# Four of 49 destination blocks summed by accumulating row gathers, b_out added to x in DRAM, finishes at uneven distances

## The reference

```python
h   = x * rsqrt(deg_out)[:, None]
agg = segment_sum(h[src], dst)                # 206250 rows of 256 numbers into 6250 sums
h   = relu((agg * rsqrt(deg_in)[:, None]) @ W + b)
gnn = h / max(norm(h), 1e-12)
mix = linear attention over all nodes, 8 heads, @ w_out + b_out
ffn = top-1 of 8 experts, capacity ceil(1.25 * 6250 / 8), two layers, 1024 hidden
```

## Time and profile before

| | |
|---|---|
| time, 3 runs | 1468.57, 1470.52, 1472.99 us; median 1470.52 |
| profiled execution, first to last instruction | 1429.1 us |
| what lies around that span (median minus span) | 41.4 us |
| busy, share of the span | PE 94%, DVE 87%, ACT 67%, POOL 45% |
| busy tenths, 40 slices of 35.7 us, PE | `4899999958999999999999999999998999899987` |
| the same, DVE | `7899999988789999999999999999976586867786` |
| granted TensorE clock, mean | 0.980 of full speed |

### The profile page before, as it was taken

How to read it: one execution, slowest core, us unless ns; L and a number is a source line. 1 busy time by engine, 2 the same in 40 slices (tenths; PEclk the granted TensorE clock), 3 DMA queues, 4 the chain that set the end, 5 groups by cost and what they waited for, 6 DMA issues and landing times. The chain is left out here.

```text
span 1429.1 us, 43152 instructions
## 1 busy us (share of the span) xinstructions
PE 1337.7 (94%) x14715; PEld 1128.4 (79%) x14717; DVE 1248.9 (87%) x2315; ACT 962.9 (67%) x2239; POOL 648.8 (45%) x645
## 2 busy tenths in 40 slices
PE   4899999958999999999999999999998999899987
PEld 3466666637899999999999999999995788889986
DVE  7899999988789999999999999999976586867786
ACT  5588888775567767677677677676663658464754
POOL 4557663062234433334433344333331676776574
PEclk9899999988999999999999999999999999999999
DMA  9211111000011111121111121111113443353220
GB/s 299 60 42 46 54 45 39 23 31 1 4 62 50 37 37 37 37 72 38 37 37 37 37 73 37 37 37 37 41 71 104 129 139 107 102 161 95 76 77 26
DMA packets 61264, 89.57 MB, mean 63 GB/s; under 512 B 10231, under 2 KB 40591, under 8 KB 61154
## 3 DMA queue, kind: packets, MB, share of 16 engines
q1 hardware_dynamic: 50032, 67.20, 13.9%
q0 software_dynamic: 11136, 21.23, 5.3%
HBM read 62.91 MB, written 34.49 MB: 68 GB/s over the span
## 5 line engine op out<-in xcount | busy, mean ns | idle before, releaser
L1621 PE MATMUL bank<-reg_b,reg_a 128*128 128x256 f16 x4802 | 642.7, 273 | 0.7 <-ACT reg_a L1206 0.7
L1206 ACT ACTIVATE reg_a<-bank 128x392 f16<-128x392 f32 x784 | 358.8, 499 | 159.2 <-PE bank L1613 154.3
L1621 PEld LDWEIGHTS bank<-reg_b,reg_a 128*128 128x128 f16 x4802 | 428.9, 97 | 42.7 <-issue 0.9
L1860 DVE TENSOR_TENSOR reg_c<-iota_v,reg_c 128x2048 f16<-128x2048 f16 (+1 forms) x298 | 432.2, 1465 | 21.6 <-PE bank L1613 11.2
L845 POOL COPY key_deg<-deg_k 128x1 f32 (+1 forms) x49 | 105.0, 2143 | 463.0 <-DVE reg_c L1989 463.0
L1613 PE MATMUL bank<-reg_a,reg_c 128*128 128x98 f16 x3136 | 261.4, 208 | 6.1 <-DVE reg_e L2069 2.2
L1613 PEld LDWEIGHTS bank<-reg_a,reg_c 128*128 128x128 f16 x3136 | 213.5, 98 | 24.9 <-issue 7.9
L1860 DVE TENSOR_TENSOR reg_a<-iota_h,reg_c 128x1568 f16<-128x1568 f16 x196 | 215.7, 1101 | 0.0
L1816 PE MATMUL bank<-w_hi,hid_hi 128*128 128x256 f32 (+1 forms) x368 | 107.3, 292 | 12.7 <-DVE w_lo L2342 7.5
L1818 PE MATMUL bank<-w_hi,hid_lo 128*128 128x256 f32 (+1 forms) x368 | 104.6, 284 | 0.0
L1817 PE MATMUL bank<-w_lo,hid_hi 128*128 128x256 f32 (+1 forms) x368 | 104.5, 284 | 0.0
(11 more groups left out here) (360 smaller groups left out, 2529.4 us busy)
## 6 DMA issues: line engine op xcount, KB each, us to landing
reg_b<-in_L_ffn_w SPq DMA_DIRECT2D x16, 1024.0 KB
tok_rows<-reg_e SPq DMA_DIRECT2D x24, 512.0 KB, 3.8
x_t<-in_x SPq DMA_DIRECT2D x24, 256.0 KB
xnT_t<-xnT_rows SPq DMA_DIRECT2D x24, 256.0 KB, 2.9
...
```

The source lines that it names most:

```text
L1206: return a.activation(AT[k].rearrange("p h (w t) -> p h w t", w=2)[:, :, :, s * GROUP:(s + 1) * GROUP], tile_ps[bk][:, 0:GROUP * 2 * NB].r ...
L1621: ins = t_.matmul(agg_ps[k][:, 0:D], AT[k][:, h, :], h_all[:, h, half * D:(half + 1) * D], start=(first and h + half == 0), stop=(last and ...
L1860: return v_.tensor_tensor(out.rearrange("p t (v u) -> p t v u", u=2), iota.rearrange("p (v u) -> p v u", u=2).unsqueeze(1).to_broadcast(sh ...
```

## The change

Four things change together.

- **Gathered blocks.** If no node needs an extra round, blocks 16, 17, 32 and 33 (pairs 8 and 16, `GATHERED`) are not summed by PE. POOL stores `h_all` to DRAM (`h_rows`, float32: the high halves, then the low ones added by accumulating DMAs, first 28 of the 49 columns of rows and then 21), and then gathers for each of the four blocks 56 times 128 rows (`GROUNDS`), one edge of each node at a time, each gather adding into one of two accumulators (`GACC`) by the DMA itself. A gather waits for the landing of the one two rounds earlier into the same accumulator, so four are in flight. DVE makes the row numbers (`gather_rows`) and adds and scales the accumulators (`gathered`). The other 45 blocks (`DENSE`) go as before. The check for extra rounds now allows 56 edges in the four blocks and 64 in the others.
- **Finishes.** The start of each finish comes from `finish_starts`, in slots: 48, 80, 112, ... 272, then 296 (pair 8), 320, 344, 368, 400, ... 496, then 520 (pair 16), 544, 568, 592, 624, ... 688. Around each gathered pair four follow at 24 slots, all others at 32. The stage is written out block by block where it was a loop of pairs.
- **Less on POOL and ACT in the finish.** DVE finishes the keys itself (two more instructions a block), takes `agg` out of PSUM with both scales in one instruction (`scaled`), and adds the bias (`biased`). POOL's three and ACT's one instruction of this go.
- **b_out.** SP copies x to `x_bias` in DRAM early on, POOL adds `b_out` to it in ten accumulating DMAs of 625 rows in the first stage (`bias_rows`), and the finishes load rows of `x_bias`.

```diff
+XB_ROWS = 250
+XB_JOIN = 5
+XB_PARTS = 10
+XB_FROM = 3
+assert N % (XB_JOIN * XB_PARTS) == 0 and XB_JOIN * D <= 2048
...
+GATHERED = (8, 16)
+GB = 2 * len(GATHERED)
+GROUNDS = 56
+GACC = 2
+GSPACE = 24
+HG = 7
+H_GROUPS = (3, 4, 0, 2, 5, 6, 1)
+DENSE = [b for b in range(NB) if b // 2 not in GATHERED]
+AT_POS = {b: p for p, b in enumerate(DENSE)}
...
+def finish_starts():
+    starts = []
+    for q in range(NQ - 1):
+        ready = 0 if q in GATHERED else (AT_POS[2 * q + 1] + 2) * SLOTS
+        starts.append(max([ready] + [s + GSPACE for s in starts[-1:]]))
+    assert all(s % CG == 0 for s in starts)
+    assert starts[NQ - 2] + 2 * SLOTS == len(DENSE) * SLOTS
+    return starts
...
+        sp.dma_start(x_bias.rearrange("(p j) d -> p (j d)", p=XB_ROWS), x.rearrange("(p j) d -> p (j d)", p=XB_ROWS)
+                     ).then_inc(xb_in, 16)
+        sp.dma_start(b_out_rows, b_out.rearrange("(a d) -> a d", a=1).to_broadcast([XB_JOIN, D])).then_inc(xb_in, 16)
...
+            part = x_bias[n * rows:(n + 1) * rows, :].rearrange("(p j) d -> p (j d)", j=XB_JOIN)
+            b_rows = b_out_rows.rearrange("(a j) d -> a (j d)", a=1).to_broadcast([rows // XB_JOIN, XB_JOIN * D])
+            g.dma_start(part, b_rows, accum_op=ALU.add).then_inc(xb_set, 16)
...
+            if i == 0 and XB_FROM <= q < XB_FROM + XB_PARTS:
+                bias_rows(q - XB_FROM)
...
-        def block_keys(b, k):
-            pool.wait_ge(key_int, b + 1)
-            apart(pool)
-            g.tensor_copy(key_deg[:, :], deg_k[:, ds(b, 1)])
-            g.tensor_copy(key_t[k][:, :, :], key_i).then_inc(key_mask, 1)
-            pool.wait_ge(key_mask, b * 2 + 1)
-            apart(pool)
-            g.tensor_scalar(key_off[:, :], iota_k[:, :], key_deg[:, :], 0.0, ALU.subtract, ALU.max).then_inc(key_mask, 1)
-            pool.wait_ge(key_mask, b * 2 + 2)
-            apart(pool)
-            g.tensor_tensor(key_t[k][:, 0, :], key_t[k][:, 0, :], key_off, ALU.add).then_inc(key_set, 1)
-
...
-            xt = fin_of(q).x[:, 0:w, :]
-            g.tensor_tensor(xt, xt, b_out_bc[:, :].unsqueeze(1).to_broadcast([P, w, D]), ALU.add).then_inc(x_added, 1)
...
-            gs = fin_of(q).g[:, 0:w, :]
-            g.tensor_tensor(gs, fin_of(q).agg[:, 0:w, :], norm_bc[:, :].unsqueeze(1).to_broadcast([P, w, D]), ALU.mult
-                            ).then_inc(fin_pool, 1)
-            pool.wait_ge(fin_pool, q + 1)
-            apart(pool)
-            g.tensor_tensor(gs, gs, gnn_b_bc[:, :].unsqueeze(1).to_broadcast([P, w, D]), ALU.add
-                            ).then_inc(fin_scaled, 2)
...
+            for ready, groups in ((26, H_GROUPS[0:4]), (N_LATE, H_GROUPS[4:])):
+                pool.wait_ge(h_lo, ready)
+                for t0 in (HG * i for i in groups):
+                    g.dma_start(out=rows[:, t0:t0 + HG, :], in_=h_all[:, 0, t0:t0 + HG, :]).then_inc(h_stored, 16)
+                stored += 16 * len(groups)
+                pool.wait_ge(h_stored, stored)
+                for t0 in (HG * i for i in groups):
+                    g.dma_start(out=rows[:, t0:t0 + HG, :], in_=h_all[:, 1, t0:t0 + HG, :], accum_op=ALU.add
+                                ).then_inc(h_stored, 16)
+                stored += 16 * len(groups)
+            pool.wait_ge(h_stored, stored)
+            landed = [[[0] * GACC for m in range(2)] for _ in range(2)]
...
+                for j in range(GROUNDS):
+                    for m in range(2):
+                        k = j % GACC
+                        if j >= GACC:
+                            pool.wait_ge(acc_in[i % 2][m][k], 16 * landed[i % 2][m][k])
+                        at = bass.IndirectOffsetOnAxis(ap=slot_src[:, 2 * q + m, j:j + 1], axis=0)
+                        if j < GACC:
+                            ins = g.indirect_dma_start(out=acc[i % 2][m][k], out_offset=None, in_=h_rows, in_offset=at)
+                        else:
+                            ins = g.indirect_dma_start(out=acc[i % 2][m][k], out_offset=None, in_=h_rows, in_offset=at,
+                                                       compute_op=ALU.add)
+                        ins.then_inc(acc_in[i % 2][m][k], 16)
+                        landed[i % 2][m][k] += 1
+
+        main_phase(pool, gnn, lambda b, s: None, lambda q, s: None, lambda q, s: None, tail, sparse)
...
-            a.activation(agg[:, k, :], agg_ps[k][:, 0:D], ACT.Copy, scale=rin[:, ds(b, 1)]).then_inc(agg_out, 1)
...
+            v_.scalar_tensor_tensor(key_t[k][:, 0, :], iota_k[:, :], deg_k[:, ds(b, 1)], key_i[:, 0, :], ALU.subtract, ALU.max)
+            v_.tensor_copy(key_t[k][:, 1, :], key_i[:, 1, :]).then_inc(key_set, 1)
...
+            v_.scalar_tensor_tensor(out_, agg_ps[k][:, 0:D], rin[:, ds(b, 1)], norm_bc[:, :], ALU.mult, ALU.mult
+                                    ).then_inc(agg_out, 1)
...
+        def gathered(i, q, gs):
+            added = []
+            for m in range(2):
+                for k in range(GACC):
+                    dve.wait_ge(acc_in[i % 2][m][k], 16 * (GROUNDS // GACC) * (i // 2 + 1))
+                for k in range(1, GACC):
+                    ins = v_.tensor_tensor(acc[i % 2][m][0], acc[i % 2][m][0], acc[i % 2][m][k], ALU.add)
+                added.append(sparse_step(ins))
+            for m in range(2):
+                dve.wait_ge(sparse_dve, added[m])
+                v_.scalar_tensor_tensor(gs[:, m, :], acc[i % 2][m][0], rin[:, 2 * q + m:2 * q + m + 1], norm_bc[:, :],
+                                        ALU.mult, ALU.mult).then_inc(acc_out, 1)
...
+            v_.tensor_tensor(gs[:, 0:w, :], gs[:, 0:w, :], gnn_b_bc[:, :].unsqueeze(1).to_broadcast([P, w, D]), ALU.add
+                             ).then_inc(fin_scaled, 2)
```

389 lines of the change are left out of this document (260 added, 129 removed).

## The result

| | before | changed |
|---|---|---|
| median of 20 runs each | 1471.28 us | 1466.05 us |
| ratio, 95% interval | | 0.9968 [0.9955, 0.9981] |
| profiled span | see below | 1462.7 us |

A forecast was written before the change was run, and what follows sets the result against it. PE was taken as the bound, with DVE nearly as full. Blocks -55.5, DVE at 24 slots +11, copy +4, additions +1, ends -2 gave -41.5 us: 1429.0 us, 2.8% faster, range 1409 to 1451.

The forecast's parts named there:

- The blocks taken away: Second stage, PE: four blocks fewer at 13.88 us each, all 25 finishes kept, -55.5 us.
- PE stays the bound at 32 slots, by 0.8 us, and nothing is lost or won: Second stage, 32-slot gaps: DVE about 29.7 us with pauses against PE's 30.5 us, so no change.
- DVE becomes the bound by 1.4 us a gap: Second stage, eight 24-slot gaps: DVE 24.9 us against PE 23.5 us; with row numbers and lead, +11 us.
- four such starts, 2 to 3 us each: Starts 296, 344, 520, 568 put two finishes' route and layernorm into one chunk's gap; part of the +24 us upper bound.
- The gathers: POOL, second stage: 112 a pair at 1.5 us each, 168 of 219 us from about 390 us; hidden, 0.
- The late rival: Gathers at a 2.55 us pitch miss their deadline by 67 us, DVE and PE stand: 1541 us; chance 0.12.
- The copy: First stage: copy of x delays the first store of transposed rows, +4 us; ten `b_out` additions on POOL, +1 us.
- The ends: Last pair's finish: DVE replaces POOL's addition, for which ACT waited 2.92 us; -2 us.
- The row numbers: DVE, second stage: made once for each gathered pair, bounded by four 687 ns instructions, within +5 us together with finish extras.
- What lies around that span, 41.4 us: Whole kernel: median taken to lie 41.4 us above the profiled 1429.1 us span, added to 1387.6 us for the forecast.

The follow-up runs named there:

- the last run: Changed kernel with early row numbers, 52 gathers a block, starts off the block's middle, addition between sums and layernorm: 1434.47 us, 0.9745 of before.
- the run with the addition between: Changed kernel with DVE's addition into `inv_acc` between the finish's sums and its layernorm, for starts at a block's beginning: 1459.48 us, 0.9933 of before.

## Why the prediction was wrong

The forecast was -41.5 us and the change gave -5. Three steps failed: the gathers put at nothing (16 us), the finishes that start in the middle of a block (20 us where 11 stood for another reason), and the 32-slot gaps put at nothing (9 us).

- **The blocks taken away: right.** The work went (45 blocks in place of 49), and with the losses mended most of the time with it: 37 us in the last run.
- **"PE stays the bound at 32 slots, by 0.8 us, and nothing is lost or won": failed.** The sum of DVE's work was right (28.3 forecast, 28.18 measured) and is not what decides. DVE and PE meet at fixed places: keys' transposes, slot products, the layernorm's halves. Between such places each engine's instructions must fit by themselves. The addition, moved behind 3.7 us of sums and layernorm, made one stretch too long; moved to the front, another. The cost was 0.6 to 1.3 us in each of 11 gaps, 9 us; the run with the addition between gives the stretches from 48 to 272, 400 to 496 and 624 to the end 9.8 us back.
- **"DVE becomes the bound by 1.4 us a gap": wrong.** Free of gathers and of block middles, 24 slots take 23.0 to 23.8 us, PE's 23.5, and DVE is busy 21.5 and 20.2 of 23.8 us: my 24.9 counted its 1.37 us of pauses as fixed work. What I kept as an upper bound, "four such starts, 2 to 3 us each", was the real mechanism and under-sized: 4.7 to 5.1 us each, 20 in all. Chunks did not run out, as I had it; about half of each is ACT waiting in its order, 1.3 and 1.7 us are the wait for the addition into `inv_acc`, and about 1 us in the first gap of each stretch goes with the lower granted clock behind PE's stop.
- **The gathers: "hidden, 0" was wrong** by 16 us. The pitch was 2.11, not 1.5, and the start at 425.4 us, not 390, since the row numbers come late; slot 296 came later, too, at 661 us on PE and not at 609. Waits of 3.2 and 4.5 us are seen at L2251. The late rival had the mechanism right: by its own window, 219 us and 11 of the ring, the limit is a pitch of 2.05, which was passed by little, so it cost some us and not 112; no row gives the 20.7 us that it adds to reach 2.2. Why each issue is long is the adding for 0.6 us and, for up to 0.4 more in the mean, what goes on beside it: with no chunk over it an adding issue took 1.60 us, with 1.5 us or more of chunks 2.04. In the changed kernel the first four of a pair, which don't add, took 0.94 and 0.95 us with no chunk over them, and 1.08 to 1.71 with one. So the two-port rule of the Trainium skill ("SBUF — State Buffer", "SBUF: two separate sides") isn't needed for the 0.6 us here. It speaks of modes of DVE that take both ports, and no row shows that the chunk instructions run in one. For an instruction with two SBUF inputs, as they are, the same section has GpSimd wait only where it reads SBUF; that the issues beside chunks are longer would agree with this, since a gather reads its row numbers there, but some adding issues took 1.54 us with chunks over all of them.
- **The copy: right in kind, its size not settled.** 4 + 1 us were forecast. ACT's wait for the store is there in every run with the copy; 5 us lie between the starts of the second stage in the two records compared, and 4 between the ratios, but these starts differ by 13 us among runs with the same copy, and the ratios' difference is no larger than their noise. That the descriptors of one ring are consumed in order, as the Trainium skill says of each DMA engine ("DMA: Bandwidth & Descriptors", "Queues, rings and completion order"), agrees with ACT's 10.35 us.
- **The ends: not shown.** -2 us were forecast, and the part behind the last block's start is 2.4 us shorter; but that is luck. ACT's wait in the last pair's finish did fall, from 2.92 to 1.15 us, yet the way from the last block's start to the third stage's first gather is as long as before, 48.0 and 47.9 us. The 2.4 us are in the third stage, which takes 322.9 to 329.2 us in the runs with `b_out`.
- **The row numbers: under-sized.** From slot 48 the changed kernel takes 37.8 us for 31.8. I had priced both pairs' row numbers at under 3 us; their place in DVE's order cost most of these 6: made two chunks earlier, the gap is 32.3.
- **The sum from the measured terms**: -55.5 + 9 (32 slots) + 20 (block middles) + 16 (gathers, with their 3 us of the first gap) + 3 (first gap, the rest) + 5 (start of the second stage) - 2 (third stage) = -4.5 us, against 5 measured. The last two terms are differences of single records.
- "What lies around that span, 41.4 us" was a misreading of one short execution. It did not move the forecast, which was a difference, but it hid that its first stage was untypical.

Open: why the first stage has executions with 10.5 us a pair and mostly others; what the copy costs at the end of that stage; how much of the 16 us of the gathers is waiting for instructions rather than for their landing; and how much of the block middles' 20 us is the clock's: no run holds the clock and changes the rest.
